# Weighing a block's values ahead of a step's last second-pass product in two attention streams

## What is computed

```python
for part in (L0_attn, L0_ffn, L1_attn, L1_ffn, L2_attn, L2_ffn, L3_attn, L3_ffn):
    h = layernorm(x) * (1 + c) + s
    x = x + g * part(h)

# L0_attn: four layers of this, with a Gelu feed-forward part behind each
# L3_attn: one such layer with rotated q and k, and no feed-forward part
scores = q @ k.T * scale + mask        # 16 heads of 8 features, causal
attn = softmax(scores)
out = (attn @ v) @ Wo.T + bo
```

## Time and profile before

| | us |
|---|---|
| median of 3 runs | 3035.25 |
| lowest, highest | 3028.97, 3037.77 |
| the profiled execution | 3035.09 |
| its span, first to last instruction | 3033.3 |

### The profile page before, as it was taken

One profiled execution on the slowest core, in us unless ns is written; L12 is line 12 of the kernel. 1 busy time (PEld: TensorE's weight loads), 2 busy tenths in 40 slices (PEclk: granted clock), 3 DMA queues, 4 the chain that ended last, 5 costly groups with the idle time before them and its releaser, 6 DMA issues. The chain is left out here.

```text
span 3033.3 us, 38272 instructions
## 1 busy us (share of the span) xinstructions
PE 2454.7 (81%) x12564; PEld 1014.7 (33%) x12564; DVE 1850.0 (61%) x4413; ACT 1391.1 (46%) x2373; POOL 548.0 (18%) x636
## 2 busy tenths in 40 slices
PE   5779989999998999998668798794556796988738
PEld 3323333333433433333233323341122342323215
DVE  3656766666676766777235675447999324867242
ACT  2345556565666556565425223335332431556420
POOL 1200111010111111010007300004796001100000
PEclk7778999999998999999868899887899795999768
DMA  2111112121122212111010000002343011112020
GB/s 92 73 61 53 65 63 74 62 74 58 60 77 77 70 54 76 59 68 51 19 34 1 21 1 25 0 9 94 117 146 112 5 39 66 64 73 70 23 84 14
DMA packets 76777, 173.15 MB, mean 57 GB/s; under 512 B 21990, under 2 KB 37606, under 8 KB 72494
## 3 DMA queue, kind: packets, MB, share of 16 engines
q1 hardware_dynamic: 76580, 170.70, 16.1%
HBM read 129.93 MB, written 39.71 MB: 56 GB/s over the span
## 5 line engine op out<-in xcount | busy, mean ns | idle before, releaser
L1062 ACT ACTIVATE sb_prob<-ps 128x512 f32<-128x512 f32 (+1 forms) x1520 | 810.3, 575 | 591.5 <-PE ps L852 382.3
L826 PE MATMUL ps<-sb_k_stack_half,sb_q_stack_half 78*128 78x512 bf16 (+3 forms) x1920 | 608.0, 351 | 116.5 <-DMA sb_q_stack_half<-alibi 43.2
L852 PE MATMUL ps<-sb_q_stack_half,sb_k_stack_half 81*128 81x128 bf16 (+2 forms) x2240 | 589.6, 321 | 65.7 <-ACT sb_prob L1062 54.2
L963 DVE TENSOR_REDUCE sb_row_max<-ps 128x1 f32<-128x512 f32 x640 | 433.7, 688 | 217.7 <-PE ps L826 216.0
L972 DVE CUSTOM_DVE_ANT_0 sb_masked_scores<-ps,sb_mask_row 128x128 bf16<-128x128 f32 (+3 forms) x640 | 284.4, 488 | 199.1 <-PE ps L826 198.3
L972 DVE CUSTOM_DVE_ANT_0 sb_masked_scores<-ps,sb_mask_row,sb_row_max 128x128 bf16<-128x128 f32 (+3 forms) x640 | 342.1, 544 | 101.7 <-PE ps L826 98.1
L852 PEld LDWEIGHTS ps<-sb_q_stack_half,sb_k_stack_half 81*128 81x128 bf16 x2240 | 205.0, 100 | 413.3 <-ACT sb_prob L1062 189.0
L873 PE MATMUL ps<-sb_prob,sb_v_first_half 128*9 128x512 f32 (+3 forms) x2560 | 315.4, 567 | 0.2 <-ACT sb_o_raw L1069 0.2
L826 PEld LDWEIGHTS ps<-sb_k_stack_half,sb_q_stack_half 78*128 78x128 bf16 x1920 | 189.3, 103 | 341.1 <-DVE sb_row_max L972 86.6
L2253 PE MATMUL ps<-sb_read_out,sb_ident 128*128 128x512 f32 x256 | 138.5, 673 | 121.3 <-DVE sb_read_out L2340 115.4
L2307 POOL TENSOR_TENSOR sb_inflow<-sb_delta_u,sb_b_spread 128x1024 f32<-128x1024 f32 x64 | 201.4, 3161 | 27.1 <-DVE sb_states L2329 19.0
(11 more groups left out here) (360 smaller groups left out, 3281.9 us busy)
## 6 DMA issues: line engine op xcount, KB each, us to landing
sb_q_stack_half<-q_rows SPq DMA_DIRECT2D x240, 96.0 KB
sb_k_stack_half<-k_rows SPq DMA_DIRECT2D x120, 192.0 KB
o_rows<-sb_o_raw SPq DMA_DIRECT2D x80, 256.0 KB, 4.1
sb_b_spread<-b_rows SPq DMA_DIRECT2D x32, 512.0 KB, 4.8
sb_c_spread<-c_rows SPq DMA_DIRECT2D x32, 512.0 KB, 3.7
sb_k_stack_half<-k_rows SPq DMA_DIRECT2D x120, 96.0 KB
q_rows<-sb_qk_parts SPq DMA_DIRECT2D x60, 128.0 KB, 2.6
k_rows<-sb_qk_parts SPq DMA_DIRECT2D x60, 128.0 KB, 2.1
```

The costliest lines, as they stand in the source:

```text
L826: pe.matmul(M.ps[:, k % RING, 0:hi - lo], qst[half][0:S1_ROWS, s, j, at:at + P], kst[half][0:S1_ROWS, s, lo // CH, j, 0:hi - lo], start=Tr ...
L852: mm = pe.matmul(bank[:, x * w + lo:x * w + hi], kst[half][0:S2_ROWS, s, t // 4, j, t % 4 * P:(t % 4 + 1) * P], qst[half][0:S2_ROWS, s, j, ...
L963: dve.reduce_max(rowmax[:, tau % 3, 0, at:at + 1], M.ps[:, k % RING, 0:w], AX_X).then_inc(first_done, 1)
L1062: act.activation(prob[:, st % PROB_STEPS, heads[0]:heads[-1] + 1, a:CH], scores.rearrange("p (j q) -> p j q", j=len(heads)), ACT.Exp).then ...
```

## The change

In a step with at least two units, TensorE issues the weighing of the step before directly ahead of the step's last unit. `behind` is then set to `None`, so that the call at the end of the step is skipped. In a step with one unit the weighing stays at the end. The last weighing of all stays where it is. The other engines' programs are the same.

```diff
@@ -928,6 +928,9 @@
                     k, last = step["first"]
                     units = step["units"]
                     for x, (kind, tau, heads, upto) in enumerate(units):
+                        if behind and x and x == len(units) - 1:
+                            weigh(*behind)
+                            behind = None
                         if kind == "turn":
                             turn(step["units_at"] + x, tau)
                         else:
```

## The result

The changed kernel takes 3089.3 us in the median of four runs (3082.46 to 3098.06), the kernel before 3033.64 in as many: a ratio of 1.0186, with an interval of 1.0155 to 1.0216. It is slower by 56 us; the prediction had 11, and a range that ended at 3062. The profiled execution took 3098.06 us, with a span of 3096.3.

What follows compares the result with a forecast made beforehand. TensorE was taken to bound both attention streams. Gains of 4.5 and 25.5 us against losses of 13.3 and 28 made +11.3 us on 3035.09: 3046 us, slower, with a range of 3018 to 3062.

Steps and rivals of the forecast that it cites:

- What bounds it, and what moves: TensorE bounds both attention streams; reordering can win only its 173 us of idle time, with instructions and count unchanged.
- Gain 1: TensorE's pauses at the Gelu: the weighing fills part, six pauses give it back before stack loads; -4.5 us.
- the push: At the Gelu: the moved weighing of the step before delays product 4, so the Gelu comes some 0.94 us later.
- a pause of 1.9 us: Sign at each Gelu: the pause should stay at 2.8 to 2.9 us; 1.9 would mean the push is wrong.
- Gain 2: Small TensorE pauses in product 4 and the first-pass products behind it are covered by the weighing: -25.5 us.
- Loss 1: In step 1 of a group the weighing waits for ScalarE to save the old output: 35 waits, +13.3 us.
- Loss 2: Product 4 and its first-pass products reach VectorE and ScalarE a weighing later, delaying bank reuse: +28 us, between 15 and 43.
- waits of first-pass products for VectorE: Sign on TensorE: waits for VectorE grow from 24 us to 35 or more; shrinking would mean Loss 2 is wrong.
- Rival 1: VectorE's idle time absorbs Loss 2, leaving about 3 us of it: 3021 us, not slower; chance 0.27.
- Rival 3: New waits for the save bring more falls of TensorE's clock, adding 20 us: 3066 us; chance 0.07.
- above 0.92: Sign in TensorE's mean granted clock: a value above this would mean the clock was the prediction's mistake.
- Rival 2: Weighing ahead of the Gelu pause keeps TensorE's clock up, 4.7 us less at eight stalls: about 3008 us; chance 0.08.

Runs made afterwards that it cites:

- gelu_only: Against the kernel before, the weighing moves only in the step behind a Gelu (15 steps by the plan); 33.8 below 3034: 3033.8 us, ratio 0.9991.
- no_side: The changed kernel, but steps that have side work keep the weighing at their end: 3014.69 us, 0.9918 of the kernel before.
- not_two: The changed kernel, but steps of two units keep the weighing at their end: 3082.46 us, 1.0135 of the kernel before.
- before_early: The kernel before, with VectorE emptying the side bank directly behind the first-pass products that TensorE issues ahead of the side work: 3008.32 us, ratio 0.991.

## Why the prediction failed

**What bounds it, and what moves:** right. Only TensorE's idle time moved, and the count of instructions stayed.

**Gain 1, the Gelu:** the push was right. In the changed kernel, at the Gelu that answers to the one of the earlier trace rows, the table load starts at 590.82, 0.54 us behind the first product of the next step; before it started 0.48 us ahead of it. So the Gelu comes 1.0 us later. That the loads take back idle time was right: gelu_only has 11.7 us more of these waits. But I expected the pause to stay at 2.8 to 2.9 us:

```profile
592.10 0.39 PE L826 MATMUL ps<-sb_k_stack_half,sb_q_stack_half 78*128 78x512 bf16 x1 [0.42 <-DVE sb_row_max L975]
592.70 0.34 PE L826 MATMUL ps<-sb_k_stack_half,sb_q_stack_half 78*128 78x384 bf16 x1 [0.21 <-DVE sb_row_max L966]
592.97 1.05 PE L873 MATMUL ps<-sb_prob,sb_v_first_half 128*9 128x512 f32 x8
595.99 0.49 PE L852 MATMUL ps<-sb_q_stack_half,sb_k_stack_half 81*128 81x512 bf16 x1 [1.98 <-ACT sb_prob L1065]
```

It is 1.98 (2.79 before), and 0.63 us stand as waits for VectorE ahead of it: nearly the same idle time, in three parts. In 12 of the 15 pauses at a Gelu in front of a second-pass product it is 1.86 to 1.98 us. I had named a pause of 1.9 us as the sign that the push is wrong. The sign was no good: no_side, without the push, has pauses of 1.80 to 1.92 at the same places, so the length doesn't tell the two apart. The start of the Gelu does.

**Gain 2, small pauses:** too large, as far as the runs tell. The two gains together, 30 us, look right beside the 34.9 us by which the steps without side work shrank in no_side. But 23.3 of these stand in the 14 steps behind a Gelu, just as in gelu_only, and have the clock in them (31.1 us less at the half clock). The other steps without side work shrank by 11.6 us, and the second stream by 4.3, where Gain 2 had 25.5. The forecast was for all steps, and no run takes the small pauses by themselves. In the changed kernel the steps without side work shrank by 16.9 us.

**Loss 1, the save:** the waits are as forecast, 10.8 us in 27 and, in the second stream, 3.2 in 10 (13.3 in 35 were expected). From the save's end to the weighing it took 0.14 us, not 0.06. As a loss of time it isn't shown.

**Loss 2, the push:** this is the step that failed. I carried the delay "up to the TensorE instruction that needs the bank next" and looked only at the banks of the two kinds of products. The side bank is a third resource of the same kind; VectorE empties it behind two products that the weighing delays, and TensorE stops at it. The code had it in front of me (`side_first`, and the wait for `side_free` at the head of each side piece). The steps with one and two units and side work grew by 35.0 us, 21.4 of it in single-unit steps, which the move doesn't touch; with VectorE's early order the same move adds 2.6 us there (+1.7 and +0.9). The sum had no wait of a side piece for its bank in it. What I did follow is there: waits of first-pass products for VectorE rose from 22.8 us in 70 to 30.4 in 108 (the forecast was 35 us or more). Put 35 to the sum and it gives 3081 us, near the 3089 measured. Part of that nearness is luck: the prediction doesn't say how much of its 28 us lay in these same steps, Gain 2 was too large, and the time at the half clock fell by 33.8 us, which gave back up to 17 us.

**The rivals.** Rival 1 (the push is absorbed) is refuted by the kernels that move the weighing in steps with side work and leave VectorE its late order. Rival 3 (more falls of the clock) is not what happened: the first stream had 218.9 us at the half clock before and 185.1 after. The granted clock of the stream rose from 0.92 to 0.94 in the stretches shown above (from 0.91 to 0.92 when both begin at 75 us); above 0.92 was to be the sign that the clock was my mistake. So Rival 2 was right in part: the 33.8 us are an estimated 17 us at most, without which the loss would be larger. Before, the product behind a pause took 0.61 us; in no_side it took 0.39 behind a pause of 1.92 us. The Trainium skill says, on the page "TensorE: Matmul & The Clock Gate", section "HAM oscillation — how this bites in real kernels", that idle gaps throttle TensorE and that the work behind them pays. These rows agree, and they show what I left open, what a pause that is filled in part does: the fall came later and was shorter. In no_side it began 1.35 us behind the start of that product and lasted 3.4 us; before, the clock had fallen 0.34 us ahead of the product, for 10.2 us. The ten us from 630.30 had a granted clock of 0.83, where the earlier trace rows has 0.51. I had argued that the pause keeps its length, and it didn't. Unlike what the rival says, this didn't outweigh the losses.

**Open.** Steps of three to five units with side work grow by 27.4 us in the changed kernel and by 18.5 with the early order. Which part of that is VectorE's queue, as in the earlier trace rows, which the waits for the save and which the clock, no run here separates. So of the 56 us the side bank is shown for some 35 to 39. The falls of the clock aren't explained one by one either: of the 7 us that not_two gave back, where its waits shrank by 25, I can only say that the half-clock time took the rest.

## What to carry to other kernels

When an instruction is moved on one engine, list every semaphore that the instructions behind it raise, and follow each through the other engines' own fixed order, up to every buffer that comes back, not only those of the moved kind. A consumer that empties a single buffer should have it ahead of work that its producer issues later. A pause that is filled ahead of a load can come back as a wait for it: in gelu_only 13.8 us went and 11.7 came. When an order is tested, test it in the old kernel as well: here it was a gain of 30 us by itself.

## What the hardware showed

Identical code outside of the two streams took from 1337 us (before_early) to 1356 us (the changed kernel, and gelu_only) in the profiled executions. Some 8 us of that stand in the very first layer norm, ahead of any changed instruction. The same eight small products and the product behind them, before and after:

```profile
27.69 1.02 PE L262 MATMUL ps<-sb_mean_weights,sb_ln_squares 128*128 128x1 f32 x8
28.58 1.10 PE L277 MATMUL ps<-sb_x_T,sb_mean_weights 128*128 128x512 f32 x2
```
```profile
27.95 1.84 PE L262 MATMUL ps<-sb_mean_weights,sb_ln_squares 128*128 128x1 f32 x8
29.66 2.05 PE L277 MATMUL ps<-sb_x_T,sb_mean_weights 128*128 128x512 f32 x2
```

1.02 and 1.84 us, 1.10 and 2.05: by their durations the full and the half clock for the same work in the same place. ("PEclk" reads 1.00 for both stretches, as the clock's records begin only at 27.66 us before and at 43.19 after.) TensorE had done the same in both until then. Five of the fourteen profiles have the short durations here, nine the long ones. With 19 us between the extremes outside of the streams, the spans of two single profiles of this kernel can't tell a difference of that size.
